# A decoder layer's attention on one core: other steps for query scores, out projection and the transposes of z

## The reference

```
kv = ln(x) @ kv_w + kv_b ;  q = ln(x) @ q_w + q_b          # 16 heads of 32
q, k = rotary(q, radius(x)), rotary(k, radius(x))           # radius = clip((x @ rh_w + rh_b)/100, .5, 2)
qn, kn = ln(q) , ln(k)                                      # per head, over 32
a = softmax(qn @ kn.T / sqrt(32)) @ v                       # per head, 512 x 512
out = a.reshape(8, 512, 512) @ out_w + out_b
x1 = x + out                                                # the layer norm follows in the next phase
```

## Time and profile before

| | |
|---|---|
| median of 3 runs | 2420.09 us (2416.45 to 2423.85) |
| the profiled execution | 2423.02 us, span 2421.0 us |
| mean granted TensorE clock | 0.901 of full speed |
| PE busy in the span | 1945.1 us (80%) |
| DVE busy | 1546.8 us (64%) |
| ACT busy | 908.2 us (38%) |
| POOL busy | 951.5 us (39%) |

### The profile page before, as it was taken

One profiled execution on the slowest core, in us unless ns is written; L12 is line 12 of the kernel. 1 busy time (PEld: TensorE's weight loads), 2 busy tenths in 40 slices (PEclk: granted clock), 3 DMA queues, 4 the chain that ended last, 5 costly groups with the idle time before them and its releaser, 6 DMA issues. The chain is left out here.

```text
span 2421.0 us, 30214 instructions
## 1 busy us (share of the span) xinstructions
PE 1945.1 (80%) x9560; PEld 1426.2 (59%) x9560; DVE 1546.8 (64%) x2943; ACT 908.2 (38%) x1532; POOL 951.5 (39%) x849
## 2 busy tenths in 40 slices
PE   4587887878888798788975799999948887788772
PEld 4455565555656465565633688888837665666651
DVE  4567667576675666767562666667654776767765
ACT  2143433334333343334341322222214555555653
POOL 1666756467564674746620222222201212221221
PEclk9688998989989898999987899999979999989985
DMA  3123132131311212222122211211031121022111
GB/s 128 26 53 87 37 94 48 48 85 36 95 47 50 77 36 74 69 57 70 38 77 101 78 53 60 79 69 53 18 107 37 52 70 49 22 69 70 53 35 52
DMA packets 90746, 148.67 MB, mean 61 GB/s; under 512 B 16560, under 2 KB 19632, under 8 KB 90672
## 3 DMA queue, kind: packets, MB, share of 16 engines
q1 hardware_dynamic: 90672, 147.76, 20.5%
HBM read 63.82 MB, written 33.55 MB: 40 GB/s over the span
## 5 line engine op out<-in xcount | busy, mean ns | idle before, releaser
L467 DVE TENSOR_REDUCE a_neg_max<-a_max 128x1 f32<-128x512 f32 x512 | 344.5, 687 | 267.3 <-PE a_max L726 258.8
L632 ACT ACTIVATE a_probs<-a_exp 128x512 f32<-128x512 f32 x512 | 290.7, 595 | 571.1 <-PE a_exp L741 568.5
L726 PE MATMUL a_max<-a_stack 96*128 96x512 f32 x512 | 235.9, 476 | 150.7 <-DMA a_stack<-a_nT_lo 100.6
L726 PEld LDWEIGHTS a_max<-a_stack 96*128 96x128 f32 x512 | 103.2, 206 | 245.4 <-DMA a_stack<-a_nT_lo 106.8
L1497 POOL TENSOR_TENSOR f_mixed<-f_tw,f_beta 128x512 f32<-128x512 f32 x64 | 96.1, 1522 | 352.2 <-DVE f_beta L1596 177.0
L311 POOL TENSOR_TENSOR a_rstd<-a_rstd,a_minus_half 128x16 f32<-128x16 f32 x64 | 186.5, 2914 | 85.0 <-DVE a_rstd L452 85.0
L703 PE MATMUL a_t<-a_w_hi,a_zT_hi 128*128 128x384 f32 x512 | 196.5, 384 | 13.4 <-DVE a_v L433 11.5
L741 PE MATMUL a_exp<-a_stack 100*128 100x512 f32 x512 | 193.5, 419 | 6.5 <-ACT a_probs L632 4.5
L704 PE MATMUL a_t<-a_w_lo,a_zT_hi 128*128 128x384 f32 x512 | 194.8, 380 | 0.0
L705 PE MATMUL a_t<-a_w_hi,a_zT_lo 128*128 128x384 f32 x512 | 193.0, 377 | 0.0
L305 POOL TENSOR_TENSOR a_n<-a_n,a_mean 128x512 f32<-128x512 f32 x64 | 67.2, 1050 | 309.8 <-DVE a_mean L441 309.6
(11 more groups left out here) (240 smaller groups left out, 4865.7 us busy)
## 6 DMA issues: line engine op xcount, KB each, us to landing
a_stack<-a_nT_hi SPq DMA_DIRECT2D x512, 64.0 KB, 2.0
a_stack<-a_nT_lo SPq DMA_DIRECT2D x256, 64.0 KB, 2.0
a_z<-x SPq DMA_DIRECT2D x8, 1024.0 KB, 7.4
a_y<-x SPq DMA_DIRECT2D x8, 1024.0 KB, 5.5
x<-a_y SPq DMA_DIRECT2D x8, 1024.0 KB, 4.4
r_xn<-x SPq DMA_DIRECT2D x8, 1024.0 KB, 5.6
r_cn<-ctx SPq DMA_DIRECT2D x8, 1024.0 KB, 7.7
x<-r_xn SPq DMA_DIRECT2D x8, 1024.0 KB, 4.3
```

What stands on the lines that cost most here:

```text
L467: nc.vector.tensor_reduce(neg_max[:, t, ROW + h:ROW + h + 1], bank_max[i % 2][:, :], AX_X, ALU.max, negate=True).then_inc(max_done, 1)
L632: nc.scalar.activation(probs[:, kt % 2, h, :], bank_exp[i % 2][:, :], ACT.Exp, scale=float(1.0 / np.sqrt(np.float32(HD)))).then_inc(exp_do ...
L726: mm(bank_max[i % 2][:, :], stack[0:ROW, par, h, t * P:(t + 1) * P], stack[0:ROW, par, HG + h, :], start=True, stop=True).then_inc(score_d ...
```

## The change

- Query scores are issued in steps 2 to 13 instead of 0 to 13, key scores one step earlier (from step 0), four project items in step 0 instead of three.
- The four `project_out` of g = 0 move from steps 10, 12, 15, 15 to 4, 5, 7, 9, all into `bank_t[1]`; their `add_out` to 4, 6, 8, 10. The projections of g = 0 then use `bank_t[0]` alone (`one = 1`), so that each tile waits for the save of the one before; in the other units they alternate as before.
- The transposes of z go into `bank_exp` and stand in steps 12, 13, 14, 15, behind the last exponentials.
- `turn_item` stands in steps 8 and 11 of g = 0, and 8 and 10 of the others (before 9 and 11); `turn_high` and `turn_low` one and two steps behind it. `weigh` in steps 5, 7, 10, 13 (before 5, 8, 11, 14). `save_qkv` by (1, 2, 4, 7) in g = 0, (2, 3, 5, 8) in the others.
- ACT issues `save_max` ahead of `z_high` of the same step.
- SP: the store of x1 stands ahead of g0's regroup, the load of y right behind it, the load of z ahead of g1's regroup, that is one unit earlier than before.
- y_sum starts at 0: the memset of `inverse` on DVE that counted it up is gone.

```diff
+KS_DONE = tuple(min(4 * (i + 1) // 3, T * HG) for i in range(16))
+QS_DONE = tuple(min(max(4 * (i - 1) // 3, 0), T * HG) for i in range(16))
+PROJECT_DONE = (4, 6, 8, 10, 12, 14, 15, 16, 16, 16, 16, 16, 16, 16, 16, 16)
+WEIGH_AT = (5, 7, 10, 13)                                             # was (5, 8, 11, 14)
+TURN_AT, SAVE_AFTER = ((8, 11), (8, 10)), ((1, 2, 4, 7), (2, 3, 5, 8))  # [g > 0]
+OUT_AT, ADD_AFTER = (4, 5, 7, 9), (4, 6, 8, 10)
+Z_AT, Z_HIGH_AT, Z_LOW_AFTER = (12, 13, 14, 15), (13, 14, 15, 15), (13, 14, 15, 15)
-X_NORM_AT, STATS_AFTER, FINAL_AFTER, SHIFT_AFTER = (5, 6, 7, 8), (6, 8, 10, 12), 6, 12
+X_NORM_AT, STATS_AFTER, FINAL_AFTER, SHIFT_AFTER = (6, 7, 8, 9), (6, 9, 11, 13), 6, 13
-TURN_HIGH_AT, TURN_LOW_AFTER = (10, 12), (11, 13)
+TURN_HIGH_AT, TURN_LOW_AFTER = ((9, 12), (9, 11)), ((10, 13), (10, 12))
...
             def unit(b, g, left, more):                    # SP
+                if g == 0 and counts(b):
+                    sp.wait_ge(y_sum, T * b)
+                    sp.dma_start(rows(x1, b - 1), y[:, :, :]).then_inc(x1_out, 16)
+                if g == 1 and more:
+                    sp.wait_ge(zT_done, T * (b + 2))
+                    sp.dma_start(z[:, :, :], rows(x, b + 2)).then_inc(x_in, 16)
                 if left >= 2:
                     regroup(G * b + g + 2, g % 2)
-                if g == 0 and counts(b):
-                    sp.wait_ge(y_sum, T * (b + 1))
-                    sp.dma_start(rows(x1, b - 1), y[:, :, :]).then_inc(x1_out, 16)
-                if g == 1:
+                if g == 0:
                     if counts(b):
                         sp.wait_ge(x1_out, 16 * b)
                     sp.dma_start(y[:, :, :], rows(x, b)).then_inc(y_in, 16)
-                    if more:
-                        sp.wait_ge(zT_done, T * (b + 2))
-                        sp.dma_start(z[:, :, :], rows(x, b + 2)).then_inc(x_in, 16)
...
             def project_item(b, g, m):                     # PE
                 U = G * b + g
                 t, k = divmod(m, K)
+                one = 1 if g == 0 else 2
                 if k == 0:
+                    if m == 0 and g == 1:
+                        pe.wait_ge(zlo_done, T * (b + 2))
+                    if t < one:
+                        pe.wait_ge(nTlo_done, 2 * (U + 1) + t + 1)
                     else:
+                        pe.wait_ge(qkv_saved, T * (U + 3) + t + 1 - one)
+                project(U + 3, (g + 3) % G, t, k, bank_t[t % one])
 
             def turn_item(b, g, left, s):
                 U = G * b + g
+                if left < 3 or g == 0 and s == 1 and not counts(b):
+                    pe.wait_ge(nTlo_done, 2 * (U + 1) + s + 1)
+                elif g == 0 and s == 1:
+                    pe.wait_ge(y_sum, T * b)
                 else:
+                    pe.wait_ge(qkv_saved, T * (U + 3) + (4 if g == 0 else 3 + s))
+                turn_heads(U + 2, s, bank_t[s])
 
             def out_item(b, t):
                 if t == 0:
                     pe.wait_ge(attnT_done, U)
+                    pe.wait_ge(nTlo_done, 2 * (U + 1) + 2)
                 else:
+                    pe.wait_ge(y_sum, T * (b - 1) + t)
+                project_out(b - 1, t, bank_t[1])
 
             def z_item(b, t):
+                if t < 2:
+                    pe.wait_ge(exp_done, T * HG * U + T * HG - 1 + t)
+                else:
                     pe.wait_ge(zlo_done, T * (b + 1) + t - 1)
                 transpose_z(b + 1, t)
...
             pe.wait_ge(attnT_done, G * B)                  # PE, the last batch entry
+            pe.wait_ge(nTlo_done, 2 * G * B)
             for t in range(T):
+                if t >= 2:
+                    pe.wait_ge(y_sum, T * (B - 1) + t - 1)
+                project_out(B - 1, t, bank_t[t % 2])
```

More of the change, by code:

```diff
@@ L510, in unit @@
                             head_var(U + 2, s, g == 2)
-                    if left >= 3 and i in SAVE_AFTER:
-                        save_qkv(U + 3, (g + 3) % G, SAVE_AFTER.index(i))
+                    if left >= 3 and i in SAVE_AFTER[g > 0]:
+                        t = SAVE_AFTER[g > 0].index(i)
+                        save_qkv(U + 3, (g + 3) % G, t, bank_t[0 if g == 0 else t % 2])
                     for s in range(2):
-                        if left >= 2 and i == TURN_LOW_AFTER[s]:
-                            turn_low(U + 2, s, bank_t[0 if g == 0 else s])
+                        if left >= 2 and i == TURN_LOW_AFTER[g > 0][s]:
+                            turn_low(U + 2, s, bank_t[s])
                     if g == 2 and more and i in STATS_AFTER:
@@ L521, in unit @@
                         x_shift(b + 2)
-                    for t in range(2):
+                    for t in range(T):
                         if g == 0 and counts(b) and i == ADD_AFTER[t]:
-                            add_out(b - 1, t)
-                    for t in range(T):
+                            add_out(b - 1, t, bank_t[1])
                         if g == 0 and left == 4 and i == Z_LOW_AFTER[t]:
                             z_low(b + 1, t)
-                    for t in range(2, T):
-                        if g == 0 and counts(b) and i == ADD_AFTER[t]:
-                            add_out(b - 1, t)
                     for c in range(T):
@@ L560, in _ @@
             for t in range(T):
-                save_qkv(0, 0, t)
+                save_qkv(0, 0, t, bank_t[t % 2])
             for s in range(2):
@@ L564, in _ @@
             for t in range(T):
-                save_qkv(1, 1, t)
+                save_qkv(1, 1, t, bank_t[t % 2])
             for s in range(2):
@@ L590, in _ @@
             for t in range(T):
-                add_out(B - 1, t)
+                add_out(B - 1, t, bank_t[t % 2])
         @block.scalar
@@ L650, in unit @@
                             square(U + 2, s)
-                        if left >= 2 and i == TURN_HIGH_AT[s]:
-                            turn_high(U + 2, s, bank_t[0 if g == 0 else s])
+                        if left >= 2 and i == TURN_HIGH_AT[g > 0][s]:
+                            turn_high(U + 2, s, bank_t[s])
+                    if i == SAVE_MAX_AT and left >= 1:
+                        save_max(U + 1, (g + 1) % 2)
                     for t in range(T):
@@ L695, in transpose_z, with project @@
                 for k in range(K):
-                    last = nc.tensor.transpose(bank_t[t % 2][:, k * P:(k + 1) * P], z[:, t, k * P:(k + 1) * P], ident[:, :])
+                    last = nc.tensor.transpose(bank_exp[t % 2][:, k * P:(k + 1) * P], z[:, t, k * P:(k + 1) * P], ident[:, :])
                 last.then_inc(zT_done, 1)
-            def project(U, g, t, k):
+            def project(U, g, t, k, bank):
                 at = slice(t * P, (t + 1) * P)
-                bank = bank_t[t % 2][:, 0:3 * GQ]
+                bank = bank[:, 0:3 * GQ]
                 mm(bank, zT_hi[:, k, at], w_hi[:, k, g, :], start=k == 0, stop=False)
@@ L754, in weigh, with project_out @@
                 last.then_inc(pv_done, 1)
-            def project_out(b, t):
+            def project_out(b, t, bank):
                 at = slice(t * P, (t + 1) * P)
-                bank = bank_t[OUT_BANK[t]]
                 for g in range(G):
@@ L836, in unit @@
                     for s in range(2):
-                        if left >= 2 and i == TURN_AT[s]:
+                        if left >= 2 and i == TURN_AT[g > 0][s]:
                             turn_item(b, g, left, s)
```

72 lines of the change are left out of this document (12 added, 60 removed).

## The result

| | before | after |
|---|---|---|
| median | 2420.5 us | 2386.95 us (2385.92 to 2388.22, 4 runs) |
| ratio | | 0.9862, 95% interval 0.9845 to 0.9879 |
| span of the profiled execution | 2421.0 us | 2385.8 us |
| attention loop | 1151.3 us | 1120.3 us |
| mean granted TensorE clock | 0.901 | 0.908 |

(The row of before is from the runs beside the changed kernel.) The change gains 33 us where 73 were forecast. The measured time lies in the range of 2285 to 2410, 40 us above the likeliest value.

The account below looks back on a forecast made before the run. No engine was full; PE's stack-transfer waits (94.1 us) and the slow clock behind them were to go. Terms: g0 +24, g1 -33 and +2.5, g2 -32, g3 -22, others; together -73, giving median 2347 us, range 2285 to 2410.

Parts of the forecast that it names:

- g0: First unit of each four-unit batch, now with all four outs: forecast 45.5 us (before 41.5), +24 over six.
- g1: Second unit of a batch, starting behind the late z splits: forecast 35.7 us (before 41.2), -33 over six.
- g3: Fourth unit of a batch, without stack wait: forecast 30.1 us (before 33.8), -22 over six.
- g2: Third unit of a batch, with four x_stats on DVE: forecast 31.0 us (before 36.3), -32 over six.
- unit 0: First unit of the attention loop, said to have neither outs nor leftover normalises: 40.4 to 35.4 us, -5.
- The price of a slow stretch: PE's matmuls at low clock behind a long idle: 2.6 us charged in g0, 2 us in g1.
- The stack wait: PE's waits for stack transfers at query scores in the loop: forecast to fall from 94 to under 15 us.
- its one idle: PE in g0 waits 5.0 us at project item 4 for save 0, behind DVE's normalise 3 and head_mean.
- D: Rival: g0's start stall keeps its clock at 1.2 GHz throughout, projections and outs twice as long; 2465 us, 7%.
- B: Rival: maxima bind, 16 query scores in 12 steps with two banks, 2 us more per unit; 2403 us, 11%.
- C: Rival: stack late again, 4.2 us of wait and 2.6 of slow clock stay in g2 and g3; 2415 us, 5%.
- its row for g0: Profile row: clock 0.54 after PE waited 2.4 us for DVE's z_low; grounds for charging g0 2.6 us.

Follow-up runs that it names:

- e9: Changed kernel, but x_stats in the loop reads 32 of the 512 columns, leaving out part of the computation: 2367.2 us, ratio 0.9767.
- e3: Changed kernel with z_high of step 14 ahead of save_max again on ACT: 2375.6 us, ratio 0.9798.
- e10: Changed kernel with 24 more matmuls, never read, on PE in g0 ahead of project item 4: 2368.1 us, ratio 0.9781.
- e6: Changed kernel with the load of z behind g1's regroup on SP again: 2390.8 us, ratio 0.9862.
- e2: Changed kernel with save 0 as DVE's first item of step 0 in g0, g2 and g3: 2356.1 us, ratio 0.9717.
- e11: e8 with 13 unread matmuls on PE ahead of g1's first project item: 2348.0 us, ratio 0.9696.
- e8: Changed kernel with e2 and e3 together, x_stats in steps 5, 7, 9, 11, and save 1 ahead of normalise 3 in g0: 2338.1 us, ratio 0.9645.

## Why the prediction was wrong

**The account.** The span was to fall by 73 and fell by 35.2, an error of 38 us. By unit (measured minus forecast level): g3 33.0 instead of 30.1 in the mean of six, +17; g2 32.5 instead of 31.0, +9; unit 0 41.4 instead of 35.4, +6; g1 36.1 instead of 35.7, +2.5; g0 45.4 instead of 45.5, -1. Another +4 is a base error: the levels were set against units 8 to 11 alone, but the six g0 before took 40.3 on average and not unit 8's 41.5 (+7), and the g2 36.9 and not 36.3 (-3.5). The rest cancels (units 26 to 29 +4, the last unit and what lies outside the loop -4).

**The step that failed** is in g2 and g3: "PE reaches project item 8 (t=2, which reuses bank 0 and waits for save 0) in step 3 at T0+5.6 and idles 2.3 us", and "These short idles are like the 2 us ones of 518 to 529 us, where the clock stayed at 1.00". The mechanism of the wait was right, down to the item, the releaser and its place; mis-sized were the idle in g3 and, in both, what follows it, which the sum put at nothing. In g3 the idle was 3.10 us in five of six units, as x_stats of step 13 delays the leftovers of the unit after it (the prediction charged its delay to g2 alone), and behind it the clock was 0.66 over 3 us. In g2 it was 1.83, less than forecast, and the clock behind it 0.55. e9 takes the tail away and g3 falls from 32.9 to 30.3: 1.2 us of this is the shorter idle (3.10 to 1.90), so about 1.4 is the clock and what follows from it. For g2, two of these kernels hold units with the same idle and no slow stretch (unit 10 of e3, unit 14 of e10, idle 1.88, clock 1.00): both take 31.0, as forecast, 1.2 less than in the change. The price of a slow stretch was charged in g0 and g1, where the idle was thought long, and not in g2 and g3; the row read in support, one stretch at 1.00 with idles of 2 us, was taken as a rule, and e6 and e9 show such idles with both outcomes.

**Partly luck: the sums of g2 and g3.** That these units take 31.0 and 30.3 at full clock, as forecast, comes from errors that cancel. PE is busy for 26.9 to 27.0 us of them (unit 11 of e9, unit 10 of e3), where 25.0 was charged, and waits for maxima only 1.5 and 2.0 us, where 2.8 and 3.7 were. And e2, which has no idle at item 8, is no shorter in g3 (30.5) than e9 with its 1.90.

**Right.** The stack wait is gone (2.1 us, bound 15). g0 has its one idle, 4.99 us against 5.0, released by save 0, and its outs wait for nothing. D does not hold: g0's clock is 0.96 and back by some 4 us behind the idle. B and C were not seen: waits for maxima total 30.3 us in 59, a_stack waits 2 in number. g0 took 45.4 us, as summed; but e10 shows that only 1.5 us of it is the slow stretch, where 2.6 was charged, so the agreement of the sum is luck by some 1.1 us. The Trainium skill (TensorE: Matmul & The Clock Gate, "Loop structure matters more than you think") calls a DVE copy out of PSUM harmless for the clock where the next matmuls follow immediately. The prediction set this against its row for g0 and followed the row; there PE idles 4.99 us until the DVE result is there, so the condition is not met, and the clock behind it is 0.57. This trace does not speak against the sentence, it shows a case that lies outside it.

**Off by a little.** g1's first project item came at T0+5.97 (457.20 less 451.23), forecast 5.4. x_stats waits for no transfer, as forecast, yet e6 shows no gain from it over the whole kernel: what g2 wins by it (1.6 us) the other units lose.

**Unit 0.** The text gave it "neither outs nor leftover normalises" and a gain of 5. It has no normalises, but its save 0 stands behind two head_means that wait for POOL, and it lost 1.0:

```profile
125.77 0.69 DVE L436 TENSOR_REDUCE a_mean<-a_n 128x16 f32<-128x512 f32 x1 [3.11 <-POOL a_n L297]
...
127.02 0.27 DVE L430 TENSOR_TENSOR a_v<-a_t,a_qkv_bias 128x128 f32<-128x128 f32 x1
```

PE idles 4.29 us until 127.35. The stretches ahead of that and behind it, both at a low clock:

```profile
115.16:127.35 12.19, 6.48 (x22) 5.09 (x20) 4.23 (x8) 3.66 (x4) 11.53 (x16) 0.64 0.26 60
127.35:135.00 7.65, 7.65 (x25) 7.07 (x26) 2.60 (x5) 2.72 (x5) 0.55 (x1) 0.60 0.44 103
```

**One bank for g0's projections was the cost of the change, and DVE's order made it one.** The forecast saw that the stall was "not removed here but moved", and took it as given. e2 shows that it was not: in the change PE stands at item 4 from T0+2.5 to T0+7.5, in e2 only to T0+3.3, so it was the place of save 0 in DVE's queue that held it.

## What to carry to other kernels

When a wait is removed, look for the next one behind the same engine's fixed queue, and ask not how busy that engine is but what stands ahead of the one instruction that frees a bank; moving one save ahead of other work of DVE gave as much again as the whole change. Charge each new idle of the TensorE, short ones too (here 1.75 to 5 us), with a chance of a slow stretch behind it. Set levels against the mean of all like units, not against one.

## What the runs showed of the hardware

- Adding 4.35 us of useless matmuls in each g0 made the kernel 20 us faster (e10), and adding 2.5 us in each g1 made it slower (e11 against e8: 12 us by the ratios, 7 us in the loops of the two traces), with the idle moved on to item 8 and the clock at 0.50 in the row behind it.
- Idles of 1.88 and 1.90 us, in neighbouring units of e9, were followed by clocks of 0.57 and 1.00. Idles of 1.75 and 1.74 us at the same query score of g2, in e2 and in the change, were followed by 0.67 and 1.00. What decides it was not found.
- Small DVE operations are not always small. In x_final of unit 7 two operations on 128x4 took 1.33 and 1.12 us, their like 0.17:

```profile
391.52 0.17 DVE L399 TENSOR_SCALAR a_rstd_x<-a_moments 128x4 f32<-128x4 f32 x1
391.60 1.33 DVE L401 TENSOR_SCALAR a_per_step<-a_per_step,a_rh_b 128x4 f32<-128x4 f32 x1
392.97 0.17 DVE L403 TENSOR_SCALAR a_per_step<-a_per_step 128x4 f32<-128x4 f32 x1
393.17 1.12 DVE L405 TENSOR_TENSOR a_per_step<-a_per_step 128x4 f32<-128x4 f32 x1
```

  PE then waited 1.30 us for the maximum behind them. In unit 11 the same two took 0.22 and 0.16 us, and two others of x_final 1.14 and 0.93. POOL was at work beside them; that it is the cause was not tested.
